# A decoder layer over four batches on one core: the last batch's experts get a deep weight ring, and its middle stage is reordered with GpSimd

## What is computed

```python
x = x + mixer(layernorm(x))      # state-space scan: 1024 channels x 16 states, gate, output projection
x = x + mlp(layernorm(x))        # per-batch weights 512x512 and 512x256, int8 "smooth quant" linears
x = x + moe(layernorm(x))        # 16 experts of inner width 128, top 2, plus a shared expert of width 512

def smooth_quant_linear(x, w):
    s  = sqrt(max(amax_over_rows(|x|), EPS) / max(amax_over_rows(|w|), EPS))
    xs, ws = x / s, w * s
    x_scale, w_scale = row_amax(|xs|) / 127, row_amax(|ws|) / 127
    return round(xs / x_scale) @ round(ws / w_scale).T * x_scale * w_scale.T

def moe(x):
    topw, sel = top_k(softmax(x @ gate_w.T), 2);  topw /= sum(topw)
    routed = sum_i topw[i] * (silu(x @ w1[sel[i]].T) * (x @ w3[sel[i]].T)) @ w2[sel[i]].T
    return routed + sigmoid(x @ shared_gate_w.T) * shared_expert(x)
```

## Time and profile before

| | |
|---|---|
| median of 3 runs | 1778.68 us (1775.83 to 1779.97) |
| profiled execution | 1779.99 us, its span 1778.3 us, granted TensorE clock 0.911 |
| busy over the span | PE 1453.5 (82%), VectorE 1363.6 (77%), GpSimd 1079.8 (61%), ScalarE 793.7 (45%) |
| DMA | 255.28 MB, mean 144 GB/s |
| after the last scan | from 1514 us to 1778.3 us: 264 us |

### The profile page before, as it was taken

One profiled execution on the slowest core, in us unless ns is written; L12 is line 12 of the kernel. 1 busy time (PEld: TensorE's weight loads), 2 busy tenths in 40 slices (PEclk: granted clock), 3 DMA queues, 4 the chain that ended last, 5 costly groups with the idle time before them and its releaser, 6 DMA issues.

```text
span 1778.3 us, 19480 instructions
## 1 busy us (share of the span) xinstructions
PE 1453.5 (82%) x5352; PEld 826.3 (46%) x5352; DVE 1363.6 (77%) x2237; ACT 793.7 (45%) x1360; POOL 1079.8 (61%) x696
## 2 busy tenths in 40 slices
PE   5935666999599899999699899997799999359772
PEld 2311222444365566444465565443665664247661
DVE  2249999956799999796899999686999997852111
ACT  3363444434834566246634465337445652220220
POOL 0079999800799899502999798304999997001001
PEclk9977777999799999999699899999799999759996
DMA  3262000312524674513536573514346765015884
GB/s 100 99 235 87 1 0 1 128 50 85 207 89 161 209 233 159 199 41 102 213 136 193 173 246 115 191 50 184 123 154 193 243 197 173 7 65 172 277 296 155
DMA packets 99018, 255.28 MB, mean 144 GB/s; under 512 B 11488, under 2 KB 11616, under 8 KB 93792
## 3 DMA queue, kind: packets, MB, share of 16 engines
q1 hardware_dynamic: 91680, 233.08, 39.4%
q0 software_dynamic: 5120, 16.78, 2.9%
q10 hardware_dynamic: 2112, 4.19, 0.6%
HBM read 211.02 MB, written 42.99 MB: 143 GB/s over the span
## 4 chain that ended last, share of the span: by engine, by line
PE 52%; DVE 20%; issue 12%; ACT 7%; POOL 4%; DMA 4%; SPq 1%; DVEq 0%; POOLq 0%; ACTq 0%
PE bank L1603 9%; DVE bank L1045 7%; PE bank L1502 6%; PE bank L1718 6%; PE bank L1512 5%; PE bank L1549 4%; PE bank L1554 4%; DMA ew_up<-in_exp_w 3%; PE bank L1543 3%; PE bank L1628 3%; PE bank L1620 2%; DVE work L1057 2%; PE bank L1520 2%; PE bank L1519 2%; DVE pairs L1057 2%
## 5 line engine op out<-in xcount | busy, mean ns | idle before, releaser
L552 POOL TENSOR_TENSOR work<-du,BB 128x1024 f32<-128x1024 f32 x256 | 603.1, 2362 | 2.3 <-DVE bank L1045 1.3
L757 ACT ACTIVATE bank<-delta,A_sb 128x512 f32<-128x512 f32 x512 | 350.9, 690 | 507.1 <-DVE pairs L1057 292.6
L1045 DVE TENSOR_TENSOR_SCAN bank<-bank,work 128x512 f32<-128x512 f32 x448 | 542.4, 1218 | 5.3 <-POOL work L552 5.2
L1603 PEld LDWEIGHTS bank<-x3T,ew_up 128*128 128x128 f32 x1984 | 295.3, 197 | 121.1 <-issue 78.7
L1603 PE MATMUL bank<-x3T,ew_up 128*128 128x128 f32 (+1 forms) x1984 | 327.6, 312 | 28.6 <-DMA ew_up<-in_exp_w 21.3
L1057 DVE TENSOR_TENSOR pairs<-bank,CB 128x512 f32<-128x512 f32 x256 | 171.8, 671 | 1.0 <-PE bank L1543 0.5
L501 POOL TENSOR_TENSOR col<-col,halfpow 128x4 f32<-128x4 f32 (+1 forms) x8 | 7.8, 972 | 218.5 <-DVE col L1163 218.5
L1057 DVE TENSOR_TENSOR work<-bank,CB 128x512 f32<-128x512 f32 x192 | 128.3, 668 | 0.0
L522 POOL TENSOR_TENSOR delta<-delta,work 128x512 f32<-128x512 f32 x32 | 47.5, 1514 | 131.2 <-ACT work L731 131.2
L1070 DVE SCALAR_TENSOR_TENSOR etm<-etm,bank 128x128 f32<-128x128 f32 (+1 forms) x124 | 38.6, 311 | 111.3 <-ACT etm L799 111.3
L1718 PE MATMUL bank<-wst,zg 128*128 128x512 f32 x256 | 117.2, 593 | 0.9 <-DVE zg L1063 0.9
(11 more groups left out here) (184 smaller groups left out, 2465.0 us busy)
## 6 DMA issues: line engine op xcount, KB each, us to landing
ew_up<-in_exp_w SPq DMA_DIRECT2D x124, 512.0 KB, 3.9
ew_dn<-in_exp_w SPq DMA_DIRECT2D x124, 256.0 KB, 4.3
hm<-xs_dram SPq DMA_DIRECT2D x92, 256.0 KB, 4.6
ys_dram<-x3T SPq DMA_DIRECT2D x92, 256.0 KB, 4.7
wst<-in_w_in SPq DMA_DIRECT2D x64, 256.0 KB, 2.8
BB<-bc_dram SPq DMA_DIRECT2D x16, 1024.0 KB, 5.1
CB<-bc_dram SPq DMA_DIRECT2D x16, 1024.0 KB, 8.2
wst<-in_out_w SPq DMA_DIRECT2D x32, 256.0 KB, 3.3
```

Of the source, the lines that this page charges most:

```text
L552: nc.gpsimd.tensor_tensor(dBu[:, k % CHUNK_SLOTS, :, :], du[:, j % 2:j % 2 + 1, :].broadcast_to([P, 2, T]), BB[:, n0:n0 + 2, :], ALU.mult) ...
L757: nc.scalar.activation(R[q % RING][:, :], delta[:, j, :], ACT.Exp, scale=A_sb[:, j, n:n + 1]).then_inc(S["da_ready"], 1)
L1045: V.tensor_tensor_scan(prod[c % (2 * PAIR_SLOTS)] if on_pool(c) else R[q % RING][:, :], R[q % RING][:, :], dBu[:, c // 2 % CHUNK_SLOTS, c ...
L1603: ins = mm(gu_bank(v)[:, part * n:(part + 1) * n], ew_up[:, q % UP_RING, part * D + k * P:part * D + (k + 1) * P], rhs, start=(k == 0), st ...
```

## The change

Outside of the last batch nothing changes.

**Experts of the last batch.** (1) The 4 shared blocks are loaded once each, 768 KB in one DMA, into `delta` and `u` as soon as the last scan's sums are done. (2) Routed weights come by one DMA of 768 KB a visit into a ring of 14 slots in `BB`, `CB` and `work`; the first 8 are issued when the routing is known, ahead of SP's wait for the scatters. (3) Rows, transposed rows and results get rings of 4 in `zg` and `pairs`. (4) The gathers go token tile by token tile, each with a semaphore of its own; combine and store (256 KB) follow by tile. (5) VectorE copies two of the four `x3T` blocks.

**Middle stage of the last batch.** (6) The first residual and its statistics start per tile; (7) `column_scales(m, 1)` moves to the last scan's end; (8) ScalarE copies the row of weight scales to SBUF (`weight_row`), and GpSimd multiplies the weights by it (`scale_weights`) instead of VectorE; (9) `scaled` writes to `x2`, and GpSimd adds the second residual of tiles 0 to 2.

```diff
+LATE_RING = 14
+LATE_ROWS = 4
+LATE_AHEAD = 8
...
+            def load_late_shared():
+                sp.wait_ge(S["nsum_done"], PAIRS * B)
+                for w in range(NSH):
+                    sp.dma_start(late_shared[w], exp_w[NE + w]).then_inc(S["late_shared_in"], 16)
+            def load_late(r):
+                if r >= LATE_RING:
+                    sp.wait_ge(S["down_done"], VISITS * (B - 1) + SHARED + r - LATE_RING + 1)
+                sp.dma_start(late_w[r % LATE_RING], expert(B - 1, SHARED + r)).then_inc(late_in[r % LATE_RING], 16)
+            def load_late_rows(r):
+                if r >= LATE_ROWS:
+                    sp.wait_ge(S["rows_ps"], ROUTED * (B - 1) + r - LATE_ROWS + 1)
...
+            def load_late_experts():
+                for r in range(LATE_AHEAD):
+                    load_late(r)
+                sp.wait_ge(S["scattered"], 16 * 2 * TT * B)
+                for j in range(ROUTED + 6):
+                    if j < ROUTED:
+                        load_late_rows(j)
+                    if j + LATE_AHEAD < ROUTED:
+                        load_late(j + LATE_AHEAD)
+                    if 0 <= j - 6 < ROUTED:
+                        store_late_rows(j - 6)
...
@@ GpSimd @@
+            def scale_weights(m, layer):
+                width, src = ((D, guw), (INT, dnw))[layer]
...
+                pool.wait_ge(S["wrow_ready"], layer + 1)
+                for t in range(TT):
+                    nc.gpsimd.tensor_tensor(src[:, t, :], src[:, t, :], wrow[:, 0:width], ALU.mult
+                                            ).then_inc(S["w_scaled"], 1)
...
+                for t in range(TT - 1):
+                    pool.wait_ge(S["linkO"], 3 * TT * m + TT + t + 1)
+                    nc.gpsimd.tensor_tensor(x2[:, t, :], x2[:, t, :], xn[:, t, :], ALU.add).then_inc(S["x2_sum"], 1)
...
+                        for s in range(LATE_ROWS):
+                            pool.wait_ge(late_ys_out[s], 16 * ((ROUTED + LATE_ROWS - 1 - s) // LATE_ROWS))
+                    for i in range(2):
+                        nc.gpsimd.indirect_dma_start(back[1 - i][t], None, ys_dram[:, :],
+                                                     bass.IndirectOffsetOnAxis(ap=posi[:, i, t:t + 1], axis=0)
+                                                     ).then_inc(late_back[t], 16)
...
@@ ScalarE @@
+            def store_late(t):
+                sc.wait_ge(S["mix_done"], 2 * TT * (B - 1) + 2 * t + 2)
+                sc.dma_start(out[B - 1][t * P:(t + 1) * P, :], back[0][t]).then_inc(S["out_done"], 16)
...
                 row_norm(m, 2 * m)
+                weight_row(m, 0)
                 magic_rows(m, 0, 0)
...
@@ VectorE @@
                         column_scales(b, 0)
+                        if b == B - 1:
+                            column_scales(b, 1)
...
-                residual(m)
-                ve.wait_ge(S["linkO"], 3 * TT * m + TT)
-                row_stats(m, 2 * m)
-                column_scales(m, 1)
...
+                first_residual(0)
+                for t in range(1, TT):
+                    first_residual(t)
+                    first_stats(t - 1)
+                first_stats(TT - 1)
...
                 q0.maxima(0)
-                q0.scale(1)
                 q0.maxima(1)
...
-                second_residual(m, q1)
-                row_stats(m, 2 * m + 1)
+                for t in range(TT):
+                    q1.scaled(t, x2[:, t, :], "linkO")
+                ve.wait_ge(S["linkO"], 3 * TT * m + 2 * TT)
+                V.tensor_tensor(x2[:, TT - 1, :], x2[:, TT - 1, :], xn[:, TT - 1, :], ALU.add).then_inc(S["linkO"], 1)
...
+                for t in (0, 1, 3, 2):
...
@@ TensorE @@
+                        w = late_shared[v % NSH] if v < SHARED else late_w[(v - SHARED) % LATE_RING]
+                        wT = late_xsT[(v - SHARED) % LATE_ROWS]
...
+                elif k == NBLK - 1:
+                    ins.then_inc(S["o_row"], 1)
```

More of the change, by code:

```diff
@@ L274, in build @@
         bcast = [sem(f"bcast{i}") for i in range(4)]
+        late_in = [sem(f"late_in{i}") for i in range(LATE_RING)]
+        late_xs_in = [sem(f"late_xs_in{i}") for i in range(LATE_ROWS)]
+        late_ys_out = [sem(f"late_ys_out{i}") for i in range(LATE_ROWS)]
+        late_back = [sem(f"late_back{i}") for i in range(TT)]
         def wait(eng, name, value):
@@ L651, in scan_stage @@
                                     scatter(i, t)
-                                if k == GATHER_AT + i:
+                                if scan and k == GATHER_AT + i:
                                     gather(i, t)
+                        if not scan and k == GATHER_AT:
+                            for t in range(TT):
+                                late_gather(t)
                     if scan and b + 1 < B and k == STATS_AT // 2 + 1:
@@ L660, in _ @@
                 scan_stage(b, True, b > 0)
-            phase1(None, B - 1)
+            last(B - 1)
             scan_stage(B, False, True)
@@ L810, in scan_stage @@
                 if experts:
-                    for i in range(KD):
+                    for i in range(KD if scan else KD // 2):
                         x3(i)
@@ L966, in _ @@
             scan_stage(B, False, True)
-            store(B - 1)
+            for t in range(TT):
+                store_late(t)
         @block.vector
@@ L1116, in scan_stage @@
                                 finish_shared(half)
-                        for i in range(2):
-                            if not scan and p == COMBINE_AT + i:
-                                combine(b - 1, i)
+                        if not scan and p == COMBINE_AT:
+                            for t in range(TT):
+                                late_combine(t)
                     if scan and b + 1 < B:
```

131 lines of the change are left out of this document (118 added, 13 removed).

## The result

The changed kernel takes 1733.23 us in the median of 4 runs (1732.36 to 1734.05), against 1778.43 us for the kernel before (4 runs, 1775.83 to 1779.97): a ratio of 0.9753, with a 95% interval of 0.9737 to 0.9768. The forecast was 1735.0. The profiled execution took 1734.05 us with a span of 1732.3, 46.0 us less than the span of before. The total was met in part by luck: terms of the sum that were too large (the shared visits and the middle stage, 7.3 us together) met gains that were forecast too small or not at all. Of all executions reported here one is slow, 1809.91 us of the kernel before in the series of e9, e11, e12 and e13; the ratios leave it out, and without it the median of that series is 1774.57 us.

What follows compares the result with a forecast made beforehand. Bounds: short dependent VectorE steps (middle stage), TensorE (shared visits), two-slot ring latency (routed visits). Terms 7.5 + 6.0 + 24.1 + 6.2 = 43.8 us less gave 1736.2 profiled, 1735 median; forecast 1730 to 1739 (0.50), low 1727, high 1749.

Steps and rivals of the forecast that it cites:

- Statistics by tile: Middle stage: residuals and statistics start per tile while TensorE still works, so they end near 1516.5; 2.4 us less.
- Column maxima moved, and the gathers: Middle stage: 1.1 us from moved maxima, given back to gathers slowed by shared weights; zero, ends 1.1 gain and 2 loss.
- Weights scaled by GpSimd: Middle stage: GpSimd takes over VectorE's weight scaling; 1.9 us less in layer 0, 1.2 in layer 1.
- Second residual: Middle stage: one addition on VectorE, three on GpSimd beside `scaled` and the first statistics; 1.2 us less, from 0.2 to 1.6.
- Copies to `x3T`: Middle stage: copies in two halves of 1.03 us on two engines instead of 2.05; 0.8 us less.
- the middle stage gives nothing: Rival: GpSimd's steps, late gathers and the wait for them take VectorE's place; 7.5 us less gain, 1742; chance 0.10.
- The shared visits: Shared expert visits: all weights are there beforehand, so a 5.71 us load and 0.33 of issue leave the chain; 6.0 less.
- The routed visits: Routed expert visits: 3.13 us each instead of 4.32, 26.6 less, minus stalls of 1.0 and 1.5; 24.1 us less.
- DMA becomes the bound: Rival, routed visits: mixed reads and writes give only 291 GB/s; 7 to 10 us of gain go, 1742 to 1746; chance 0.22.
- Scatters starve: Rival, routed visits' start: scatters land late beside weights, TensorE stands still 3 to 5 us, 1738 to 1740; chance 0.15.
- The end: After the last gather lands: two short operations and a 256 KB store; 10.0 us become 3.8, 6.2 less.
- Slower than before: Rival: rows queued behind weights hold DMA to 180 GB/s, 124 us instead of 86, about 1781; chance 0.01.

Runs made afterwards that it cites:

- e9: The changed kernel unaltered, run once more as yardstick on another chip: 1732.73 us beside 1774.57 for the kernel before, ratio 0.9759.
- e11: The kernel before with the small VectorE product at each batch's head split into four one-column operations: 1776.05 us, ratio 1.0004.
- e12: The changed kernel with all repairs: two semaphores, small operations by columns, half a combine moved later, last residual read from PSUM: 1731.96 us, ratio 0.9754.
- e13: The changed kernel with 14 slots for routed weights but one load ahead instead of 8: 1732.54 us, ratio 0.9755.
- e3: The changed kernel with the shared weights loaded only after batch 2's gathers have landed: 1730.93 us, ratio 0.9751.
- e8: The changed kernel with 1152 instead of 1024 bytes for GpSimd's DMA descriptors: 1734.47 us, one run.
- e4: The kernel before with the small product at each batch's head moved from VectorE to GpSimd, as two operations: 1777.71 us, ratio 1.002.
- e10: The changed kernel with two semaphores instead of one for each batch's gathers and scatters, four transfers on each: 1730.20 us, ratio 0.9753.
- e6: The changed kernel with the old end: gathers in the old order, combines behind the last landing, one 1 MB store: 1736.72 us, ratio 0.9792.

## Why the prediction was right, and which of its steps were not

**Statistics by tile**: 2.4 forecast. From TensorE's first output product to the aggregate it was 8.76 us and is 6.33: 2.43. Right.

**Column maxima moved, and the gathers**: zero forecast, from 1.1 of gain to 2 of loss; measured a loss of 3.0 (10.48 us from the aggregate to the reduce, 7.51 before), outside these ends. The failed step is "the eighth lands at 1518 to 1519.6": it kept the gather's issue where it was and moved only the landing, though the prediction itself had the eighth scatter go out when the seventh had landed. In the trace of after the landing took 6.47 us, close to the 6.1 that I had taken, but the issue itself came 2.3 us later behind the seventh, whose landing took 5.9 us instead of 3.6. By the test of "what would make me wrong" (a combine that stands still for over 3 us) this step is wrong, with 4.60.

**Weights scaled by GpSimd**: 1.9 and 1.2 forecast, measured 1.54 (10.61 to 9.07) and 1.09 (6.34 to 5.25). What is missing in layer 0 is the row at 1534.77: a VectorE operation on 128x4 numbers took 1.16 us beside GpSimd's multiplications.

**Second residual**: 1.2 forecast, 1.37 measured (from the end of `scaled` to the aggregate, 4.94 to 3.57). The addition on VectorE took 1.11 us, so it was held up a little but not for a whole GpSimd operation of 1.39. That the term came out is partly luck: in e3 and e8, where the products ahead ran at a clock of 0.50, the same addition took 1.82 and 1.81 us, and the gain was 0.7 (4.28 and 4.27 instead of 4.94). The prediction's 0.2 us, an estimate from the Trainium skill (SBUF — State Buffer, Who interferes with whom: the two engines exclude each other) with GpSimd always first, is below both.

**Copies to `x3T`**: 0.8 forecast, 2.10 to 1.34 measured, 0.76. Right. These items give 2.43 - 2.97 + 1.54 + 1.09 + 1.37 + 0.76 = 4.2 of A's 4.95. The other 0.7 is no step of the change: layer 1's products and `scaled`, at the higher clock shown above, gave 0.95, and small losses between the items took 0.2 back. The rival "the middle stage gives nothing" had the right mechanism, late gathers, and cost about 3 of its 7.5.

**The shared visits**: 6.0 forecast, 1.25 measured (C). This is the step that failed outright: "the chain holds a load of 5.71 us ... 6.0 us less". The chain's piece was real, but it wasn't time in which TensorE stood still. The stretch of before holding it (columns as in the earlier trace rows) and TensorE's wait for these weights:

```profile
1612.20:1644.70 32.50, 31.78 (x122) 22.81 (x123) 6.35 (x16) 1.92 (x5) 8.14 (x10) 1.00 0.64 219
...
PE bank L1603 <- DMA ew_up<-in_exp_w: 0.7, 2, 0.4
```

The same stretch in the changed kernel:

```profile
1600.80:1632.10 31.30, 31.28 (x122) 23.03 (x123) 6.39 (x16) 1.92 (x5) 8.19 (x10) 1.00 0.86 321
```

TensorE was busy for 31.78 of 32.50 us, and waited 0.7 for the weights, in two waits of 0.36. A wait cost more than its own length: by the starts of their products the three visits around the two waits took 16.8 us (1613.97 to 1630.74) where three others take 15.5 (5.17 each). These 1.25 us are all that C gave, and the earlier trace rows with 50.5 of 53 us busy had already said that 6.0 was too much: only 2.5 were idle in all.

**B**, which I did not forecast, gave 1.66 us by TensorE's clock. The router's products, in before and in after:

```profile
1592.30:1598.40 6.10, 6.08 (x32) 6.08 (x33) 0.00 (x0) 1.27 (x1) 0.00 (x0) 0.57 0.01 3
```

```profile
1582.60:1588.20 5.60, 5.58 (x33) 5.58 (x34) 0.02 (x1) 1.05 (x1) 0.00 (x0) 0.65 0.01 3
```

The granted clock was 0.57 and is 0.65, between its levels of 1.2 and 2.4 GHz, and the 13 us behind them went from 0.82 to 0.88. The change need not be the cause: e4, with the router code of before, has 0.67 and 18.2 us. B is 18.2 us in eight of the kernels and 19.9 to 20.2 in six; e12, whose middle stage gave more, lost 2 us here. The engine comes out of a stage in which it did little (28.4 us of 73.1), and at which moment the clock rises isn't set by anything that the change aims at.

**The routed visits**: 24.1 forecast, 26.4 measured (D). The 26.6 us of the visits' pace were right: 3.09 us a visit where I took 3.13. The two deductions for stalls, 1.5 for DMA that falls behind and 1.0 at the start, were not needed: TensorE waited 0.4 us in all for rows, in one wait. The stretches of after where DMA is fullest:

```profile
1652.00:1664.00 12.00, 11.62 (x82) 9.61 (x81) 2.30 (x8) 4.51 (x12) 0.00 (x0) 1.00 1.02 375
1632.00:1660.00 28.00, 27.30 (x189) 22.29 (x188) 6.18 (x18) 9.68 (x24) 0.00 (x0) 1.00 0.96 360
```

I had sized DMA at 345 GB/s, from 291 at a share of 0.89 and one stretch at 363. It gave 360 over 28 us and 375 over 12. With 1.31 MB a visit, 360 GB/s is 3.6 us, more than TensorE's 3.09: this stretch does fall behind, but the eight loads ahead and the last visits without loads make up for it. e13, without the loads ahead, moves its extra weights at 361 GB/s and doesn't wait either. The rival "DMA becomes the bound" is refuted.

*Scatters starve*: by half. The timeline of the last scatter, and the row load behind it on SyncE's queue:

```profile
1618.96 0.95 POOL L691 DMA_INDIRECT xs_dram<-xn,posi  x1 [9.30 <-issue]
...
1625.32 0.33 SPq L467 DMA_DIRECT2D zg<-xs_dram  x1
```

The eighth scatter waited 9.30 us instead of 5.68. But the first rows could go out at 1625.32, and the first transposes came at 1631.91, 6.6 us later and straight behind TensorE's shared visits, with no wait for rows. The delay is there and nobody waits for it. By the Trainium skill (DMA: Bandwidth & Descriptors, Queues, rings and completion order) the queues share each DMA engine packet by packet; the landings that grow beside weights (6.47 us for the gather, 3.3 alone) agree, while e10 shows that a good part of the lateness was the eighth's wait for landings counted on its semaphore, not its own time on the engines.

**The end**: 6.2 forecast, 7.0 measured. The timeline of its last operations:

```profile
1723.55 0.95 POOL L715 DMA_INDIRECT ew_up<-ys_dram,posi  x1 [0.30 <-issue]
1728.26 0.75 DVE L1221 SCALAR_TENSOR_TENSOR hm<-hm,tw,x 128x512 f32<-128x512 f32 x1 [0.39 <-DMA ew_up<-ys_dram,posi]
1729.05 0.75 DVE L1224 SCALAR_TENSOR_TENSOR ew_up<-ew_up,tw,hm 128x512 f32<-128x512 f32 x1
```

From 1728.26 to the span's end are 4.0 us, against the 3.8 that I had worked out. Against e6, combine and store by tile are worth 4.7 us. The eighth gather's wait, 3.29 us before and 0.30 now, is the other part; I had taken for granted that it stays.

*Slower than before.* The arithmetic of this rival doesn't hold: 124 us "instead of 86" is 38 more, and with the other terms' 19.7 gained the sum is 1798, not 1781. From the eighth scatter's landing at 1629.9 to the last row transposes at 1735.6 the kernel before took 106 us, which would give 1778. DMA gave 360 GB/s, not 180, so nothing rests on it.

**In sum**: A 2.5 less than forecast, C 4.75 less, B 1.7 more, D 2.3 more, E 0.8 more, and 4.75 us more ahead of the last batch's middle stage, from the stall in the profiled execution of before. That the total came out so near is luck: 7.3 us too much in two terms, and on the other side 3.1 us in two terms, the 1.7 of the clock and the 4.75. The medians differ by 45.2 us, in e9's series by 41.8; the forecast was 43.8. Right was the main thing: two slots set the pace of the routed visits, and with enough slots TensorE sets it.

## What to carry to other kernels

- A transfer on the chain of waits isn't idle time of the engine behind it. Before booking it as a gain, read how long that engine really stood still in the stretch: its busy time against the length, and its own waits.
- If rows and weights go out from one list, a deeper ring helps by keeping every wait in the list fulfilled; at 5 slots one held queue cost the whole gain while DMA had 0.39 of its time free. What was tested is the ring, not another order of the list.
- When transfers are moved to where others run, ask for the issue of those others too, not only for their landing. Eight indirect transfers on one semaphore made the eighth wait for the seventh's landing; with four on each of two it waited for the fourth's, which for the gathers had long come.

## What the runs showed that I had not expected

- **Eight indirect transfers on one semaphore.** The eighth went out after 3.3 to 5.6 us of idle time on GpSimd (gathers) and 9.30 (scatters). Each time it went out some 0.6 us after the seventh had landed. With four on each semaphore (e10) or two (the end of after and of e6) the gathers' wait was 0.30 us. A descriptor buffer of 1152 instead of 1024 bytes took no wait away.
- **Small VectorE operations beside GpSimd.** A 128x4 operation with two inputs in SBUF took 7.2 us once each in three profiled executions, and 0.15 to 0.88 elsewhere; in before it ended with the last of four GpSimd operations, and its batch took 6 us longer. Even one with a single 128x4 input took 1.16 us instead of 0.17. By the Trainium skill (SBUF — State Buffer, Who interferes with whom) the two engines exclude each other for an instruction; here VectorE's waited for four in a row (7.2 us).
- **The rate of mixed transfers.** Loads and stores together moved 375 GB/s for 12 us, with TensorE busy 97% of the time beside them.
- **The clock's share.** Two microseconds of B and one of A depended on the granted clock of the router's and of layer 1's products, as much as most of the single repairs gave, and it differed between kernels with the same code in these stages.
